# Attention of a two-layer kernel: weights split once per turn on ScalarE and VectorE, a copy moved to ScalarE, and TensorE's slots 6 and 8 in another order

## The reference

```python
# 16 heads of 128, 16 segments of 64 tokens; in 4 turns of 4 heads in the kernel
sigma_q, sigma_k = elu(q) + 1.0, elu(k) + 1.0
att_dot = softmax(causal(q @ k.T / sqrt(128))) @ v              # inside a segment
att_mem = sigma_q @ mem / (sigma_q @ z)                          # from the segments before
delta   = v - sigma_k @ mem / (sigma_k @ z)
mem     = mem + sigma_k.T @ delta;  z = z + sum(sigma_k)
out     = (beta * att_mem + (1 - beta) * att_dot) @ Wo
```

## Time and profile before

| | us |
|---|---|
| median of three runs | 691.3 (691.24 to 692.1) |
| profiled execution | 690.62 |
| its span | 688.7 |
| outside the span | 1.9 |
| busy: PE, PEld, DVE, ACT, POOL | 617.8, 523.3, 417.9, 353.4, 291.3 |

### The profile page before, as it was taken

How to read it: one execution, slowest core, us unless ns; L and a number is a source line. 1 busy time by engine, 2 the same in 40 slices (tenths; PEclk the granted TensorE clock), 3 DMA queues, 4 the chain that set the end, 5 groups by cost and what they waited for, 6 DMA issues and landing times. The chain is left out here.

```text
span 688.7 us, 12915 instructions
## 1 busy us (share of the span) xinstructions
PE 617.8 (90%) x4390; PEld 523.3 (76%) x4390; DVE 417.9 (61%) x1076; ACT 353.4 (51%) x845; POOL 291.3 (42%) x357
## 2 busy tenths in 40 slices
PE   3888999999999999999999999778799968996796
PEld 3767888988987987997987989667455546986553
DVE  6858478179269169269269264569545459635554
ACT  3665776566566566566566566132356621301242
POOL 4675462643633543544544111160477523401454
PEclk9999999999999999999999999989999979998799
DMA  8111011010111110010010013289233253008731
GB/s 255 52 39 56 26 37 32 31 39 32 32 39 32 32 38 30 30 38 30 30 40 1 1 45 81 69 297 411 78 102 100 78 171 147 1 1 288 244 92 35
DMA packets 28723, 55.28 MB, mean 80 GB/s; under 512 B 4254, under 2 KB 15488, under 8 KB 28672
## 3 DMA queue, kind: packets, MB, share of 16 engines
q1 hardware_dynamic: 22720, 42.03, 17.9%
q0 software_dynamic: 3840, 10.49, 5.0%
q10 hardware_dynamic: 2112, 2.10, 0.9%
HBM read 46.35 MB, written 8.78 MB: 80 GB/s over the span
## 5 line engine op out<-in xcount | busy, mean ns | idle before, releaser
L915 DVE RECIPROCAL denominators<-readings 128x2 f32<-128x2 f32 x128 | 21.2, 166 | 147.4 <-PE readings L591 146.4
L451 POOL TENSOR_TENSOR w_high<-xn,ones 128x256 fp32r<-128x256 f32 x84 | 53.8, 672 | 76.8 <-PE ahead L239 35.5
L591 PEld LDWEIGHTS readings<-memory_copy,sigma 128*128 128x128 f32 x512 | 75.4, 191 | 11.4 <-ACT memory_copy L788 2.3
L788 ACT ACTIVATE memory_copy<-memory 128x258 f32<-128x258 f32 x128 | 50.3, 393 | 62.1 <-PE memory L601 48.1
L797 ACT ACTIVATE memory_reading<-readings,denominators 64x128 f32<-64x128 f32 x256 | 78.5, 356 | 6.0 <-DVE denominators L915 4.0
L591 PE MATMUL readings<-memory_copy,sigma 128*128 128x129 f32 x512 | 78.8, 276 | 2.2 <-ACT memory_copy L788 2.1
L921 DVE SCALAR_TENSOR_TENSOR minus_delta<-readings,denominators,v 64x128 f32<-64x128 f32 x240 | 73.8, 346 | 4.5 <-DVE denominators L915 0.3
L601 PE MATMUL memory<-minus_delta,sigma_k_tokens 128*128 128x129 f32 x480 | 73.3, 275 | 0.0
L773 ACT ACTIVATE x<-ahead 128x512 f32<-128x512 f32 x60 | 35.8, 597 | 62.5 <-PE ahead L239 28.8
L455 POOL TENSOR_TENSOR w_low<-xn,w_high 128x256 fp32r<-128x256 f32 x84 | 65.6, 812 | 1.7
L640 PE MATMUL ahead<-wo,attT 128*128 128x256 f32 x256 | 64.5, 396 | 1.0 <-DVE attT L950 1.0
(11 more groups left out here) (300 smaller groups left out, 1537.2 us busy)
## 6 DMA issues: line engine op xcount, KB each, us to landing
weights_e<-experts SPq DMA_DIRECT2D x24, 608.0 KB, 12.4
xn<-L_attn_Wq SPq DMA_DIRECT2D x8, 512.0 KB, 3.9
xn<-L_attn_Wk SPq DMA_DIRECT2D x7, 512.0 KB, 3.8
xn<-L_attn_Wv SPq DMA_DIRECT2D x7, 512.0 KB, 3.9
wo<-L_attn_Wo SPq DMA_DIRECT2D x1, 2048.0 KB, 13.7
rows_e<-xn ACTq DMA_DIRECT2D x4, 512.0 KB, 9.8
x<-L_attn_x SPq DMA_DIRECT2D x4, 256.0 KB, 3.7
x<-L_attn_x SPq DMA_DIRECT2D x2, 512.0 KB, 3.6
```

What stands on the lines that cost most here:

```text
L451: last = pool.tensor_tensor(w_high[i][:, :, of], w_stage[:, :, of], one, ALU.mult)
L591: last = pe.matmul(KQ[g][:, hh * MC:(hh + 1) * MC], sqk[:, GROUP * g + hh, pair, 2 * par:2 * par + 2, :], mz[g][:, hh, :], start=True, sto ...
L788: act.activation(mz[g][:, :, :], MM[g][:, 0:GROUP * MC].rearrange("p (h c) -> p h c", h=GROUP), ACT.Copy).then_inc(mem_copied[g], 1)
```

## The change

- There are three pairs of weight buffers (q, k, v), and a set is split once in a turn, for both halves. ScalarE writes the high part (`weights_high`, 128x1024, in slots 6, 12 and 14 of a turn's first half), VectorE the low part (`weights_low`, slots 11, 13 and 15). GpSimd only splits k and v at the start. Weights are loaded once in a turn, k into a staging tile of its own.
- To make room, `kT` holds one half only, and so does `qT` for two of the four heads; the copies of projections 6 and 7 wait for the stage's second `scores`.
- The copy of sigma of k from `sk` to `sqk` goes from VectorE to ScalarE (`place_sigma_k`, slots 7 to 10, three slots behind its projection), except at the start. The Exp of projections 6 and 7 and the transposes wait for `sk` instead of for that copy.
- In TensorE's slots 6 and 8 the work of the table (`AHEAD_AT`) stands ahead of `scores` and of `turn_probs`.

```diff
-w_high = [sb(f"w_high{i}", [P, KD, HQ * DK], F32R) for i in range(2)]
-w_low = [sb(f"w_low{i}", [P, KD, HQ * DK], F32R) for i in range(2)]
+w_high = [sb(f"w_high{i}", [P, KD, HQ * DK], F32R) for i in range(3)]
+w_low = [sb(f"w_low{i}", [P, KD, HQ * DK], F32R) for i in range(3)]
...
-qT, kT = carried.space, sb("kT", [P, HQ, T])
+kT = sb("kT", [P, HQ, HALF])
+space = carried.space[:, :, :].rearrange("p h t -> p (h t)")
+k_staged = space[:, 3 * T:4 * T].rearrange("p (k n) -> p k n", k=KD)
+
+def qT(h, half):
+
+    begin = h * HALF if h < 2 else (h - 1) * T + half * HALF
+    return space[:, begin:begin + HALF]
 
...
+SPLIT_HIGH_AT, SPLIT_LOW_AT = {6: 0, 12: 1, 14: 2}, {11: 0, 13: 1, 15: 2}
...
-        load_weights(Wq, 0, 1)
-        load_weights(Wk, 0, 4)
 
         def turn(it, first, last):
-            load_weights(Wv, it, 6 * it + 5)
+            if not last:
+                load_weights(w_staged, Wq, it + 1, 3 * it + 3, w_loaded)
+                load_weights(k_staged, Wk, it + 1, 3 * it + 3, k_loaded)
             if not first:
                 store_out(it - 1, 0, 2 * it - 2)
             if not last:
-                load_weights(Wq, it + 1, 6 * it + 6)
-                load_weights(Wk, it + 1, 6 * it + 7)
-                load_weights(Wv, it + 1, 6 * it + 8)
+                load_weights(w_staged, Wv, it + 1, 3 * it + 4, w_loaded)
             if not first:
                 store_out(it - 1, 1, 2 * it - 1)
-            if not last:
-                load_weights(Wq, it + 1, 6 * it + 9)
-                load_weights(Wk, it + 1, 6 * it + 10)
...
-        def stage(n, first=False, value_weights=True, key_weights=True):
-
-            if value_weights:
-                pool.wait_ge(low_done, 3 * n + 5)
-            else:
-                pool.wait_ge(p_ready, 4 * n)
+        def stage(n, first=False):
+
             shift_scores(2 * n)
-            if value_weights:
-                pool.wait_ge(shifted, 2 * n + 1)
-                pool.wait_ge(proj_ready, 12 * n + 16)
-                split(0, 3 * n + 6)
-                pool.wait_ge(low_done, 3 * n + 6)
             probabilities(2 * n, not first)
             pool.wait_ge(p_ready, 4 * n + 2)
             shift_scores(2 * n + 1)
             probabilities(2 * n + 1)
-            if key_weights:
-                pool.wait_ge(p_ready, 4 * n + 4)
-                pool.wait_ge(proj_ready, 12 * n + 24)
-                split(0, 3 * n + 7)
-                split(1, 3 * n + 8)
+            pool.wait_ge(p_ready, 4 * n + 4)
 
         pool.wait_ge(low_done, 1)
-        split(1, 2, 0)
-        pool.wait_ge(proj_ready, 4)
-        split(0, 3, 1)
+        split_at_start(1)
+        pool.wait_ge(low_done, 2)
+        split_at_start(2)
         pool.wait_ge(low_done, 3)
         set_constants()
-        pool.wait_ge(proj_ready, 12)
-        split(0, 4)
-        split(1, 5)
         stage(0, True)
-        with pool.Fori(0, STAGES - 3) as i:
+        with pool.Fori(0, STAGES - 1) as i:
             stage(i + 1)
-        stage(STAGES - 2, False, True, False)
-        stage(STAGES - 1, False, False, False)
         norm.invert(pool, 1, 0)
...
             if u % 4 == 0:
-                pe.wait_ge(low_done, 3 * n + u // 4 + 1)
+                pe.wait_ge(low_done, 3 * group + u // 4 + 1)
...
-            pe.wait_ge(sigma_ready, 8 * n + h + 5)
+            pe.wait_ge(sk_ready, 4 * n + h + 1)
             for t in range(TPH):
...
@@ -649,11 +630,6 @@
                 if behind:
                     pe.wait_ge(bt_copied, 4 * n - 1)
                 scores(n, half, 0)
-            if m == 6:
-                if behind:
-                    pe.wait_ge(att_ready, 4 * n)
-                pe.wait_ge(masked, 2 * n + 1)
...
                 turn_reading(1 - half, h)
-            if m == 8:
-                pe.wait_ge(p_ready, 4 * n + 2)
-                pe.wait_ge(masked, 2 * n + 2)
...
-                    project(n + 1, 1 - half, u, free)
+                    project(n + 1, it + half, 1 - half, u, free)
+            if m == 6:
+                if behind:
+                    pe.wait_ge(att_ready, 4 * n)
+                pe.wait_ge(masked, 2 * n + 1)
+                scores(n, half, 1)
+            if m == 8:
+                pe.wait_ge(p_ready, 4 * n + 2)
+                pe.wait_ge(masked, 2 * n + 2)
+                turn_probs(n, 0, 0)
+                turn_probs(n, 0, 1)
             out_at = OUT_AT if ahead else LAST_OUT_AT
...
                 n = 2 * it + half
-                pe.wait_ge(sigma_ready, 8 * n + 8)
+                pe.wait_ge(sigma_ready, 4 * n + 4)
...
-                if u >= 2:
-                    act.wait_ge(sigma_ready, 8 * n + u - 1)
+                if 2 <= u < 6:
+                    act.wait_ge(sigma_ready, 4 * n + u - 1)
+                elif u >= 6:
+                    act.wait_ge(sk_ready, 4 * n + u - 5)
                 act.activation(e[u % 2][:, :], bank[:, :], ACT.Exp)
-                act.activation((qT, kT)[u // 4][:, u % 4, half * HALF:(half + 1) * HALF], bank[:, :],
-                               ACT.Copy).then_inc(qk_copied, 1)
+                if at_start is None and u >= 6:
+                    act.wait_ge(sc_ready, 2 * n)
+                act.activation(kT[:, u % 4, :] if u >= 4 else qT(u, half), bank[:, :], ACT.Copy)\
+                   .then_inc(qk_copied, 1)
...
+
+        def place_sigma_k(n, half, h):
+
+            act.wait_ge(sk_ready, 4 * n + h + 1)
+            act.activation(sqk[:, h, half * TPH:(half + 1) * TPH, 0:4:3, :],
+                           sk[h % 2][:, :].rearrange("p (t a c) -> p t a c", a=2, c=SEG), ACT.Copy)\
+               .then_inc(sk_placed, 1)
...
+        def weights_high(it, half, m, last):
+
+            if last or half or m not in SPLIT_HIGH_AT:
+                return
+            i = SPLIT_HIGH_AT[m]
+            if i == 1:
+                act.wait_ge(k_loaded, 16 * it + 16)
+            else:
+                act.wait_ge(w_loaded, 32 * it + (32, None, 48)[i])
+            act.wait_ge(proj_ready, 24 * it + 12 + 4 * i + 4)
+            act.activation(w_high[i][:, :, :], (k_staged if i == 1 else w_staged)[:, :, :], ACT.Copy)\
+               .then_inc(high_done, 1)
...
+            if not (last and half):
+                for what, u in AHEAD_AT.get(m - 3, ()):
+                    if what == "project" and 4 <= u < 8:
+                        place_sigma_k(n + 1, 1 - half, u - 4)
 
         def slot(it, half, m, first, last):
...
                     copy_memory(it, 1, s)
                     scale_reading(it, 0, s)
+                    place_ahead(it, half, 2 * at, last)
                     slot(it, half, 2 * at, first, last)
...
-        def sigma(n, half, u):
...
+                    dve.wait_ge(sk_placed, 4 * n + u - 5)
                 dve.scalar_tensor_tensor(out=sk[h % 2][:, :], in0=natural, scalar=0.0, in1=e[u % 2][:, :],
                                          op0=ALU.max, op1=ALU.add).then_inc(sk_ready, 1)
-                dve.wait_ge(sk_ready, 4 * n + h + 1)
-            tiles = slice(half * TPH, (half + 1) * TPH)
-            if i:
-                last = dve.tensor_copy(sqk[:, h, tiles, 0:4:3, :], by_segment(sk[h % 2][:, :]))
+                if at_start:
+                    dve.wait_ge(sk_ready, 4 * n + h + 1)
+                    dve.tensor_copy(sqk[:, h, tiles, 0:4:3, :], by_segment(sk[h % 2][:, :])).then_inc(sk_placed, 1)
             else:
-                last = dve.scalar_tensor_tensor(out=sqk[:, h, tiles, 1:3, :], in0=by_segment(natural), scalar=0.0,
-                                                in1=by_segment(e[u % 2][:, :]), op0=ALU.max, op1=ALU.add)
-            last.then_inc(sigma_ready, 1)
+                dve.scalar_tensor_tensor(out=sqk[:, h, tiles, 1:3, :], in0=by_segment(natural), scalar=0.0,
+                                         in1=by_segment(e[u % 2][:, :]), op0=ALU.max, op1=ALU.add)\
+                   .then_inc(sigma_ready, 1)
 
...
 
+        def weights_low(it, i):
+
+            dve.wait_ge(high_done, 3 * it + 4 + i)
+            dve.tensor_tensor(w_low[i][:, :, :], (k_staged if i == 1 else w_staged)[:, :, :],
+                              fr(w_high[i][:, :, :]), ALU.subtract).then_inc(low_done, 1)
...
                 set_beta(it)
+            if m in SPLIT_LOW_AT and not half and not last:
+                weights_low(it, SPLIT_LOW_AT[m])
```

More of the change, by code:

```diff
@@ L440, in _, with split_at_start @@
                 heads = [slice(h * DK, (h + 1) * DK) for h in range(HQ)]
-                def split(i, n, start=None):
-                    if start is not None:
-                        pool.wait_ge(start_loaded[start], 16)
-                        w_stage = at_start[start]
-                    else:
-                        pool.wait_ge(w_loaded, 16 * n - 32)
-                        w_stage = w_staged
+                def split_at_start(i):
+                    staged = at_start[i - 1]
+                    pool.wait_ge(start_loaded[i - 1], 16)
                     for of in heads:
```

(22 more changed lines are left out.)

28 lines of the change are left out of this document (14 added, 14 removed).

## The result

The changed kernel takes 685.9 us (median of 11 runs), the kernel before in the same runs 693.2. The ratio is 0.9901, 95% interval 0.988 to 0.9921: 1.0% faster, 6.9 us by the ratio and 7.3 between the medians. The forecast was 683.2 on a kernel before of 691.3, a ratio of 0.988.

A forecast was written before the change was run, and what follows sets the result against it. TensorE bounds the attention, so only its waits can be saved. Start -1.6, stage 0's weights -1.9, stage 0 -3.1, six stages -1.5: -8.1 on 690.6 gives 682.5, median 0.7 above, 683.2 us; range 676 to 688.

The forecast's parts named there:

- Start, -1.6: Before stage 0: a third buffer pair lets GpSimd split v without waiting for the fourth projection, saving 1.6 us.
- Stage 0, -1.9 - 3.1 = -5.0: Stage 0: 1.9 us of weight waits vanish; shorter waits in slots 6 to 8, no low clock and slot 10 give -3.1.
- The splits at nothing: Weight splits moved to ScalarE and VectorE, mostly in slots 11 to 15, cost nothing because both engines wait for TensorE there.
- Slots 6 to 8, 11.94 to 11.2: Stages 1 to 6: these three slots together fall from 11.94 to 11.2 us, a gain of 0.7 a stage.
- Slot 10's +0.45: Slot 9's placement on ScalarE delays the copies of the probabilities, so TensorE waits 0.45 us longer in slot 10.
- The placement, 0.62: ScalarE's copy of sigma of k takes 0.62 us, bounded by 0.43 and 1.06.
- the third rival: The placement on ScalarE is dear: at 1.3 us it costs 9.5 us and gives 692.7; chance 0.05.
- VectorE 0.65 earlier without GpSimd's splits: Slots 4 to 6: with GpSimd's splits gone, VectorE's sigma of q runs faster and VectorE is about 0.65 us earlier.
- In slot 6 projection 6 goes first and covers the 0.80.: Slot 6: the new order hides TensorE's 0.80 us wait for the reading's addition; slot 7 begins at 210.4, not 211.33.
- the new wait of slot 8: Slot 8: transposes, now first behind the update, wait 0.95 us for ScalarE's copy of projection 7, which `turn_probs` had covered.
- In stage 7, without projections, and behind the attention I expect no difference.: Stage 7 and everything after the attention: no change in time, so nothing in the sum.
- The fourth rival: Six stages gain, but the start's gain is lost to a clock falling elsewhere; no own chance, others 0.02.

The follow-up runs named there:

- splits_only: Changed kernel with TensorE's old order and the copy of sigma of k back on VectorE, keeping new splits and waits; 684.7 us, 0.989 of the kernel before.
- order_back: Changed kernel with TensorE's slots 6 and 8 put back in the old order; 680.3 us, 0.9832 of the kernel before.
- slot8_back: Changed kernel with only TensorE's slot 8 put back in the old order; 679.9 us, 0.9824 of the kernel before.

## Why the prediction was right, and where it was not

**Start, -1.6.** Measured -1.0 with the fast beginning and -2.2 with the slow one; the forecast lies between. With the fast one 0.79 us of the wait for v's low part are left where it had 0.4, with the slow one nothing.

**Stage 0, -1.9 - 3.1 = -5.0.** Measured -5.4. The waits for weights gave 1.25 in slot 0 and 1.11 in slots 3 and 4, together 2.4. Slot 8 fell from 7.85 to 4.11 with the low clock gone, and slot 10 rose by 0.46. `splits_only` has nearly the same stage 0 (43.67 us, after 44.15), so neither the order nor the moved copy is needed for this gain.

**The splits at nothing.** Held in stages 1 to 6 (slots 11 to 15 differ by at most 0.02 us, also in stages 2 and 4, which hold splits). It missed 0.40 us in stage 0, whose slots are shorter: slot 13 took 2.05 for 1.65, and the readings' longest wait for the memory copy is 0.9 us. ScalarE there, after, and TensorE behind it:

```profile
73.90 1.06 ACT L834 ACTIVATE w_high<-carried 128x1024 fp32r<-128x1024 f32 x1
74.98 0.39 ACT L781 ACTIVATE memory_copy<-memory 128x258 f32<-128x258 f32 x1
...
75.42 0.71 PE L572 MATMUL readings<-memory_copy,sigma 128*128 128x129 f32 x4 [0.89 <-ACT memory_copy L781]
```

This is the second split, and it stands right ahead of slot 13's memory copy.

**Slots 6 to 8, 11.94 to 11.2.** Measured 11.30, with the three waits of the text: 0.47 in slot 7 (0.5), 0.87 in slot 8 (0.95), 0.39 in slot 10 (0.45). Slot 10's +0.45 is exact. Slot 9 gave 0.13 that wasn't foreseen. A stage gained 0.32 instead of 0.25.

**The placement, 0.62.** Measured 0.63 to 0.64. The Trainium skill (Trainium Architecture — The Big Picture, section The five engines, in one table) has VectorE up to about three times as fast per element, from which the estimate of 1.29 came; here ScalarE takes 1.5 times VectorE's 0.43, and the third rival falls with that.

**VectorE 0.65 earlier without GpSimd's splits.** It was, by 0.64 (`sk` ready 5.02 us after slot 6's start for 5.66): `sigma` of q takes 0.69 where it took 0.99 and 1.11, and the stage's first `sk` still takes 1.42, beside GpSimd's probabilities. After, VectorE and GpSimd:

```profile
200.46 0.69 DVE L925 SCALAR_TENSOR_TENSOR sigma<-carried,x 128x512 f32<-128x512 f32 x1
...
204.29 1.42 DVE L919 SCALAR_TENSOR_TENSOR sigma_k<-kT,x 128x512 f32<-128x512 f32 x1
```

```profile
202.94 2.22 POOL L481 TENSOR_TENSOR xn<-scores,exp_sum_inverse 64x512 f32<-64x512 f32 x2 [11.48 <-DVE exp_sum_inverse L961]
```

The Trainium skill (SBUF — State Buffer, section SBUF: two separate sides) says that a VectorE operation with two inputs in SBUF and a GpSimd operation that reads SBUF shut each other out; the rows agree in direction: 0.69 alone, 1.42 with a GpSimd row of 2.22 us beside it.

**What failed: "In slot 6 projection 6 goes first and covers the 0.80."** The length was right and the reason wrong. VectorE's lead takes that wait away without the reorder: `order_back` has slot 6 at 3.70 with the old order, and `splits_only` at 3.68. The working gave VectorE's lead to `sk` and left the reading's addition, which stands on the same engine, where it was. It also priced the new wait of slot 8 at 0.95 without asking what the old order would have cost there: 3.66 us and not 4.59, by `slot8_back`. So the forecast of the time came out right, while the change holds a part, slot 8's order, that loses 5 of the 12 us that the rest would give. Its sum never compared the parts with each other, only each with the kernel before.

**What failed: "In stage 7, without projections, and behind the attention I expect no difference."** Stage 7 is the same. Behind it the profiled pair differs by 2.4 us, and the three executions of the changed kernel lie 1.5 to 2.7 above the two of the kernel before. The fourth rival had a loss at a falling clock elsewhere, and got no chance of its own since no wait of the attention spoke for it; part of this loss is of that kind, behind the attention. Here the forecast was lucky as well: stages 0 to 6 gained 7.3 us where it had 6.5, and the loss took more than the difference back. The start's gain, hidden in the profiled pair, is why the profiled executions differ by only 5.0 us; with like beginnings the pieces (1.0 to 2.2, and 7.3, less 1.5 to 2.7) come to 5.6 to 8.0, and the medians differ by 7.3. The median's forecast was 2.7 too low, of which 1.9 is the kernel before itself, 693.2 in these runs and 691.3 in the three shown.

## What to carry to other kernels

When work is taken off an engine, recompute every wait that this engine released before adding a reorder that is to cover one of them: here the lead of VectorE had already closed the wait, and the reorder only opened another. A moved copy and a new order must be tried apart and together, since the same copy gained 0.46 us a stage under one order and lost 0.20 under the other. And an engine that looks a third idle over the attention (ScalarE, busy for 34.6 of 50 us) can be full in the one slot where the next engine waits for it.

## What the hardware did that I had not expected

TensorE's speed at the start of the program differs between executions of one program: the first ten matmuls start 0.43 us apart in some and 0.23 in others, worth 0.8 (22.00 for 21.20, after) to 2.1 us (24.24 for 22.16, before). Behind the attention two executions of `splits_only` differ by 4.2 us. Together that is well above 0.2% of this kernel (1.4 us), so a single pair of profiled spans can't show a difference of a few microseconds, while the slots of stages 1 to 6 agree between executions of a kernel to within 0.04 us.
